# The recurrent stage of a GRU plus attention kernel is rebuilt: input part accumulated in PSUM, rows normed in row layout, no loop

## The reference, cut to what matters

```python
# x: (16, 128, 256) = B, T, D;  cond: (16, 256)
def cell(h, x_t):                                  # GRU, 128 serial steps
    i_r, i_z, i_n = split(x_t @ W_ih + b_ih, 3)    # W_ih, W_hh: (256, 768)
    h_r, h_z, h_n = split(h @ W_hh + b_hh, 3)
    r, z = sigmoid(i_r + h_r), sigmoid(i_z + h_z)
    n = tanh(i_n + r * h_n)
    return (1 - z) * n + z * h
x = x + scan(cell, cond, x over T)                 # stage 1

ada = cond @ ada_w + ada_b                         # shift1, scale1, gate1, shift2, scale2, gate2
x1 = layernorm(x) * (1 + scale1) + shift1
q, k, v = split(x1 @ qkv_w + qkv_b)                # 16 heads of 128, softmax over T = 128
y = x + gate1 * (attention(q, k, v) @ out_w + out_b)
x2 = layernorm(y) * (1 + scale2) + shift2
y = y + gate2 * (gelu(x2 @ ffn_w1 + ffn_b1) @ ffn_w2 + ffn_b2)
return x + y
```

## Time and profile before

| what | value |
|---|---|
| runs | 914.82, 917.31, 920.45 us |
| profiled execution: its own time | 920.45 us |
| its span, first to last instruction | 920.4 us |
| PE busy | 812.1 us (88%) |
| DVE busy | 621.4 us (68%) |
| ACT busy | 509.5 us (55%) |
| POOL busy | 162.2 us (18%) |
| mean granted TensorE clock | 0.881 of 2.4 GHz |

### The profile page before, as it was taken

How to read it: one execution, slowest core, us unless ns; L and a number is a source line. 1 busy time by engine, 2 the same in 40 slices (tenths; PEclk the granted TensorE clock), 3 DMA queues, 4 the chain that set the end, 5 groups by cost and what they waited for, 6 DMA issues and landing times.

```text
span 920.4 us, 29171 instructions
## 1 busy us (share of the span) xinstructions
PE 812.1 (88%) x11135; PEld 587.1 (64%) x11135; DVE 621.4 (68%) x1550; ACT 509.5 (55%) x1625; POOL 162.2 (18%) x267
## 2 busy tenths in 40 slices
PE   4985858888588878999999999999999999989998
PEld 3974747767577755676666766667766667744443
DVE  4475757777577766767767777676776778755562
ACT  3253535454345436666666666666666676664544
POOL 0043434444345430000001000000000100010130
PEclk9576767776667659999999999999999999999999
DMA  6011111112110000000000000000000000000001
GB/s 220 8 49 41 46 42 44 41 41 77 39 48 18 0 2 2 1 1 0 0 1 0 0 0 0 0 0 0 0 0 1 1 2 1 1 1 23 23 0 46
DMA packets 13257, 18.86 MB, mean 20 GB/s; under 512 B 2724, under 2 KB 9992, under 8 KB 13192
## 3 DMA queue, kind: packets, MB, share of 16 engines
q1 hardware_dynamic: 13192, 17.90, 6.4%
HBM read 15.79 MB, written 2.10 MB: 19 GB/s over the span
## 4 chain that ended last, share of the span: by engine, by line
PE 66%; DVE 14%; issue 11%; ACT 5%; SPq 1%; DMA 1%; POOL 1%; DVEq 1%; ACTq 0%; POOLq 0%
PE bank L382 15%; PE bank L384 15%; PE bank L383 15%; PE bank L501 14%; DVE nu L1068 3%; DVE h_hi L1074 3%; PE bank L635 3%; ACT zg L808 2%; DVE hs L1076 2%; DVE h_lo L1079 1%; DMA xin<-in_x 1%; PE bank L393 1%; DVE hid_lo L1156 1%; PE bank L403 1%; PE bank L458 1%
## 5 line engine op out<-in xcount | busy, mean ns | idle before, releaser
L501 PE MATMUL bank<-h_hi,whh_hi 128*128 128x16 f16 x1536 | 114.8, 178 | 19.5 <-DVE h_hi L1074 16.2
L382 PE MATMUL bank<-y_hi,w_hi 128*128 (+3 forms) x324 | 122.6, 379 | 2.4 <-DVE y_lo L1107 1.6
L383 PE MATMUL bank<-y_hi,w_lo 128*128 (+3 forms) x324 | 122.6, 379 | 0.0
L384 PE MATMUL bank<-y_lo,w_hi 128*128 (+3 forms) x324 | 122.4, 379 | 0.0
L501 PEld LDWEIGHTS bank<-h_hi,whh_hi 128*128 128x128 f16 x1536 | 93.7, 101 | 30.4 <-DVE h_hi L1074 29.6
L501 PE MATMUL bank<-h_hi,whh_lo 128*128 128x16 f16 x1536 | 112.3, 176 | 0.0
L806 ACT ACTIVATE zr<-bank 128x32 f32<-128x32 f32 x128 | 25.7, 201 | 138.7 <-PE bank L501 137.8
L884 ACT ACTIVATE prob<-bank,nmx 128x128 f32<-128x128 f32 x256 | 90.2, 364 | 10.8 <-DVE nmx L1166 10.8
L501 PEld LDWEIGHTS bank<-h_hi,whh_lo 128*128 128x128 f16 x1536 | 94.2, 102 | 0.0
L501 PE MATMUL bank<-h_lo,whh_hi 128*128 128x16 f16 x1536 | 79.7, 177 | 12.8 <-DVE h_lo L1079 12.0
L1183 DVE SCALAR_TENSOR_TENSOR kT_lo<-bank,bT,kT_hi 128x512 f16<-128x512 f32 x64 | 48.0, 750 | 63.6 <-ACT kT_hi L894 63.5
(11 more groups left out here) (177 smaller groups left out, 2451.0 us busy)
## 6 DMA issues: line engine op xcount, KB each, us to landing
stage<-in_L_cond_qkv_w SPq DMA_DIRECT2D x16, 384.0 KB, 4.8
xin<-in_x SPq DMA_DIRECT2D x128, 16.0 KB, 1.8
adaw<-in_L_cond_ada_w SPq DMA_DIRECT2D x1, 1536.0 KB, 7.4
stage<-in_L_cond_out_w SPq DMA_DIRECT2D x4, 384.0 KB, 3.5
out<-ynat SPq DMA_DIRECT2D x3, 512.0 KB, 3.0
wg<-in_L_cond_W_ih SPq DMA_DIRECT2D x1, 768.0 KB, 4.2
wg<-in_L_cond_W_hh SPq DMA_DIRECT2D x1, 768.0 KB, 5.8
stage<-in_L_cond_ffn_w SPq DMA_DIRECT2D x2, 384.0 KB, 3.6
```

What stands on the lines that cost most here:

```text
L382: mm(ps, w[0], a[0], start=start, stop=False, skip_group_check=True)
L383: mm(ps, w[1], a[0], start=False, stop=False, skip_group_check=True)
L384: return mm(ps, w[0], a[1], start=False, stop=stop, skip_group_check=True)
L501: mm = nc.tensor.matmul(out(m), half[:, k, w], a, start=False, stop=not high, skip_group_check=True)
```

## The change

The recurrent stage, its prologue and the layout of `xr` are rewritten; attention and feed-forward keep their order.

- **Gates.** Each gate has two PSUM banks that alternate by block. Bias products (with a broadcast operand) and the x_tile products of block r + 1 go straight into them, the recurrent products of the step add to them. `grz`, `gnb` and the products and evictions that moved them are gone. In a step, two z products stand ahead of the wait for `h_lo`. The n bank interleaves the hidden and the input part (every second column).
- **One place per step.** After a step's own work each engine has at most one or two pieces of other work, listed by s. x tiles come at steps 5, 6 and 7, the bias products at 1 and 2, the x transposes at 3.
- **Rows.** x is loaded with one transfer a block, partition = batch * 8 + time. The sum goes straight into `xr`, whose last axes are now (block, batch, time in the block). Mean and variance by bn_stats and bn_aggr on DVE, pow on GpSimd, two operations on DVE for scale and shift in row layout with rows of modulation, transposes back, y high and low out of PSUM in runs of eight times.
- **GpSimd** keeps the weight pieces (256 columns, five a block, each behind the step's `h_lo`) and the pow. x_low and y_low are on DVE.
- **No loop.** All 16 blocks are written out on all engines.
- **Prologue.** The small transfers are issued by ACT; the gate matrices come in halves by k and are split in quarters; the modulation is computed as rows in block 0 (shift1, scale1) and as columns in block 15 (the other eight tiles).

```diff
-        grz = [sb(f"grz{i}", [P, 2, BS, 2 * GB], f16, gru) for i in (0, 1)]
-        gnb = [sb(f"gnb{i}", [P, 2, BS, GB, 2], f16, gru) for i in (0, 1)]
...
+        r_bank, z_bank, n_bank = (bank[0], bank[3]), (bank[1], bank[6]), (bank[2], bank[7])
+        n_cols = [ps[:, :].rearrange("p (t j s) -> p t j s", t=BS, s=2) for ps in n_bank]
+        x_ps = bank[4][:, 0:D].rearrange("p (k c) -> p k c", k=KD)
+        row_ps, back_ps = bank[5][:, 0:D], bank[5][:, D:2 * D].rearrange("p (k c) -> p k c", k=KD)
...  # SP
+                sp.dma_start(xin[:, n % 2, :], x[:, n * BS:(n + 1) * BS, :]).then_inc(x_in[n % 2], 16)
+            def load_pieces(r):
+                for i in range(PB):
+                    sp.dma_start(stage[:, r % 2, i, :], pieces[r * PB + i]).then_inc(stage_in[r % 2], 16)
+            sp.dma_start(wih32[:, 0, :], wih_v[:, 0, :]).then_inc(wih_in[0], 16)
+            load_x(0)
+            sp.dma_start(wih32[:, 1, :], wih_v[:, 1, :]).then_inc(wih_in[1], 16)
...
+            for r in range(NBL - 1):
+                if r > 0:
+                    sp.wait_ge(piece_lo, r * PB)
+                load_pieces(r + 1)
+                if r + 2 < NBL:
+                    sp.wait_ge(xt_T, r + 1)
+                    load_x(r + 2)
...  # GpSimd
+            def piece_low(j, t1):
+                pool.wait_ge(piece_hi, j + 1)
+                pool.wait_ge(hlo_ok, t1 + 1)
+                r, i = j // PB, j % PB
+                gtt(w_lo[:, j * PC:(j + 1) * PC], stage[:, r % 2, i, :], w_hi[:, j * PC:(j + 1) * PC], sub
+                    ).then_inc(piece_lo, 1)
-            with pool.Fori(1, NBL - 2, 2) as r:
-                gru_block(r, 1)
-                gru_block(r + 1, 0)
+            for r in range(NBL):
+                for i, s in enumerate((1, 2, 5, 6, 7)):
+                    piece_low(r * PB + i, r * BS + (s + 1))
+                    if r > 0 and s == 2:
+                        pool.wait_ge(hlo_ok, r * BS + 5)
+                        rows_rstd(r - 1)
...  # TensorE
+            def x_bias(ps, at, width):
+                for half, first in ((bb_hi, True), (bb_lo, False)):
+                    nc.tensor.matmul(ps[:, 0:BS * width], ident16[:, :],
+                                     half[:, at:at + width].unsqueeze(1).broadcast_to([P, BS, width]), start=first,
                                      stop=False, skip_group_check=True)
...  # a step
-                pe.wait_ge(oz_ok, t1)
-                for ps, c in ((rb, 0), (zb, GB)):
...
+                pe.wait_ge(hhi_ok, t1)
+                high(0)
+                high(4)
+                high(2, slice(0, 2))
                 pe.wait_ge(hlo_ok, t1)
+                low(0).then_inc(r_mm, 1)
+                low(4).then_inc(hn_mm, 1)
+                high(2, slice(2, 8))
+                low(2).then_inc(z_mm, 1)
+            for r in range(NBL):
+                for s in range(BS):
+                    gru_step(r, s)
+                    if r > 0 and s == 0:
+                        rows_T(r - 1)
+                    if r > 0 and s == 4:
+                        rows_back(r - 1)
+                    if r < NBL - 1:
+                        if s == 1:   bias_rz(r + 1)
+                        elif s == 2: bias_n(r + 1)
+                        elif s == 3: x_block_T(r + 1)
+                        elif s == 5: (wait xt_lo) x_tile(r + 1, 0), x_tile(r + 1, 1)
+                        elif s == 6: x_tile(r + 1, 2), x_tile(r + 1, 3)
+                        elif s == 7: x_tile(r + 1, 4), x_tile(r + 1, 5)
+                    if r == 0 and s == 3:          row_modulation(0)
+                    elif r == 0 and s == 4:        row_modulation(1)
+                    elif r == NBL - 1 and s in (1, 2, 3, 4):
+                        modulation(range(2 * s + 2, 2 * s + 4))
...  # ACT, after a step's tanh
+                    if s in (0, 1, 2, 4, 6):
+                        piece_high(r * PB + (0, 1, 2, 4, 6).index(s))
+                    elif s == 3 and r < NBL - 1:
+                        x_full(r + 1)
+                        x_high(r + 1)
+                    elif s == 5 and r > 0:
                         y_high(r - 1)
...  # DVE
+            def x_low(n):
+                dve.wait_ge(xt_hi, n + 1)
+                tt(xb_lo[:, :, :].rearrange("p k (t b) -> p k t b", b=B), x_ps.rearrange("p k (b t) -> p k t b", b=B),
+                   xb_hi[:, :, :].rearrange("p k (t b) -> p k t b", b=B), ALU.subtract).then_inc(xt_lo, 1)
+            def rows_sum(n):
+                tt(xr[:, :, n, :].rearrange("p k (b t) -> p k b t", b=B),
+                   x32[:, n % 2, :, :].rearrange("p k (b t) -> p k b t", b=B),
+                   hs[:, n % 2, :, :, 1].rearrange("p t (k b) -> p k b t", b=B), ALU.add).then_inc(xr_ok, 1)
+            def rows_scale(n):
+                stt(ra[:, :], row_ps, mvb[:, 0:1], scale_rows[:, :], ALU.subtract, ALU.mult).then_inc(lb_a, 1)
+            def rows_shift(n):
+                stt(rb[:, :], ra[:, :], rsb[:, :], shift_rows[:, :], ALU.mult, ALU.add).then_inc(lb_b, 1)
+            row_work = {0: rows_sum, 1: rows_stats, 2: rows_var, 3: rows_scale, 4: rows_shift, 6: y_low}
+                    if r > 0 and s in row_work:
+                        row_work[s](r - 1)
+                    if r < NBL - 1 and s == 5:
+                        x_low(r + 1)
...  # residual (L1206); L361, L364 and L1232 in the same way
-                    op = tt(xr2[:, k, quad, :], gated[:, k, :, :], xr[:, k, quad, :], ALU.add)
+                    op = tt(by_block(xr2[:, k, quad, :]), by_block(gated[:, k, :, :]), xr_v[:, k, quad, :, :], ALU.add)
```

More of the change, by code:

```diff
@@ new lines, in _, with gru_step, high, low @@
+            bias_rz(0)
+            bias_n(0)
+            pe.wait_ge(xt_lo, 1)
+            for k in range(KD):
+                pe.wait_ge(wih_l, 2 * k + 2)
+                for m in range(GM):
+                    x_tile(0, m, (k,))
+            pe.wait_ge(whh_l, 2 * KD)
+            def gru_step(r, s):
+                t1 = r * BS + (s + 1)
+                rows = [(m, k, half) for m in range(2) for k in range(KD) for half in (whh_hi, whh_lo)]
+                def high(m0, part=slice(None)):
+                    for m, k, half in rows[part]:
+                        w = slice((m0 + m) * P, (m0 + m + 1) * P)
+                        nc.tensor.matmul(out(m0 + m), half[:, k, w], h_hi[:, k * B:(k + 1) * B, 1], start=False,
+                                         stop=False, skip_group_check=True)
+                def low(m0):
@@ L496, in gate @@
                     for m in range(2):
                         for k in range(KD):
-                            w = slice((m0 + m) * P, (m0 + m + 1) * P)
-                            a = h_hi[:, k * B:(k + 1) * B, 1] if high else h_lo[:, k * B:(k + 1) * B]
-                            for half in (whh_hi, whh_lo) if high else (whh_hi,):
-                                mm = nc.tensor.matmul(out(m), half[:, k, w], a, start=False, stop=not high,
-                                                      skip_group_check=True)
@@ L803, in gru_block @@
+            for k in range(KD):
+                gate_high(whh_hi, whh32, whh_in, whh_h, k)
+            for r in range(NBL):
                 for s in range(BS):
@@ L1048, in rows_shift @@
-            def rows_shift(n):
-                dve.wait_ge(lb_m, n + 1)
-                dve.wait_ge(lb_lo, n + 1)
-                modulate(yb, ym[:, :, :].rearrange("p k c -> p (k c)"), SH1, ALU.add, lb_y, n)
-            for half in (0, 1):
-                rz_low(0, 0, half)
-            nb_low(0, 0)
-            def gru_block(r, par, rows, ahead):
+                    tt(dst[:, :, :], ada[:, gate_tile:gate_tile + KD, :], spread(bT[:, bias:bias + KD], KD), ALU.mult
+                       ).then_inc(ada_ok, 1)
@@ L1080, in gru_block @@
-                    if s == 0 and not (isinstance(r, int) and r == 0):
-                        rz_low(r, par, 1)
-                    if rows:
-                        if s == 0:
-                            for k in range(KD):
-                                rows_sum(r - 1, 1 - par, k)
-                        elif s in rows_stage:
-                            rows_stage[s](r - 1)
-                    elif s == BS - 1:
-                        modulation()
-                    if ahead and s == 4:
-                        nb_low(r + 1, 1 - par)
@@ L1110, in rows @@
+            for work in row_work.values():
+                work(NBL - 1)
             def rows(g, j):
```

615 lines of the change are left out of this document (242 added, 373 removed).

## The result

The changed kernel took 933.91 us (median; its runs 933.09 to 934.83) beside 916.07 us for the kernel before on the same chip: a ratio of 1.021, 95% interval 1.014 to 1.028. (The ratios here leave out runs that lie more than 1.5% above the fastest of their kernel, so they can differ by up to 1% from the quotient of the medians.) The forecast was 856 us. The change made the kernel slower by about 2%, and the prediction missed by 78 us.

The account below looks back on a forecast made before the run. Bound: latency of the 128 serial steps, plus 63.0 us of excess from block 0, loop stops and GpSimd contention. The terms sum to -63.9 from the profiled 920.4, giving 856.5 us, stated as 856; range 845 to 887.

Parts of the forecast that it names:

- Part 4: Gates: removed per-step products worth 0; x tiles in steps 5 to 7 cost 0 to +9 us, taken +4.5.
- Part 6: VectorE's one work per step between h_lo and npre, window about 0.67 us: 0 to +31 us, taken +1.
- rival A: Strided reads are slow: steps 0 and 5 of each block grow by 0.75 and 1.35 us; +31, 887 us; chance 0.12.
- Part 1: Recurrent loop written out as 16 blocks, so no stops at the jump: -22.5 us.
- Part 2: Work leaves GpSimd and its weight pieces are released by h_lo, so nu is clear of contention: -32.7 us.
- Part 3: Block 0: 18 modulation products leave, -7.8 us; two row-shaped ones come in, 0 to +1.8, taken +1.
- Part 5: Two z products ahead of the h_lo wait in each step: 0 to +6.8 us in 128 steps, taken +1.
- Part 7: Block 15 takes eight modulation tiles, two per step: 0 to +1.8 us, taken +1.5.
- Part 8: Prologue: small transfers on ACT's queue, first h_hi at 13.8 to 14.3 us; -7 us, between -4 and -8.
- Part 9: Tail, up to the first last-block product: 10.3 us become about 7.4, so -2.9 us.
- Part 10: SP's issues per block fall from ten to six, 0; attention stage sums in runs of 8 floats, 0 to +8 us, taken 0.
- D: Written-out code can't be fetched in time, TensorE waits at block ends: +131, 987 us; chance 0.04.

Follow-up runs that it names:

- a: Changed kernel with rows_T issued after step 1's products instead of step 0's; 918.47 us, ratio 1.014.
- b: Changed kernel with rows_back issued after step 5's products, ahead of the tiles, instead of after step 4's; 917.97 us, ratio 1.014.
- c: Changed kernel with the six input tiles issued three each after steps 6 and 7 instead of two each after 5, 6, 7; 919.73 us, ratio 1.016.
- d: The rebalanced kernel: changed kernel with recurrent-stage work dealt out anew so no between-step TensorE wait is for same-step VectorE work; 861.86 us, ratio 0.952.
- e: Kernel before with rows_T moved from step 2 to step 0; 943.49 us, ratio 1.043.
- f: Kernel before with its recurrent-stage loop over pairs of blocks written out on all four engines; 914.42 us, ratio 1.011.
- g: d with GpSimd's five weight pieces a block no longer waiting for h_lo; 882.14 us, ratio 0.975.
- j: Changed kernel with input tiles 4 and 5 writing neighbouring columns instead of every second one, output wrong; 927.76 us, ratio 1.018.
- k: i with the two z products put back behind the low products of r and n; 852.95 us, ratio 0.935.
- i: d with the eight small loads issued ahead of the weights, four on SyncE's queue and four on ScalarE's; 857.20 us, ratio 0.947.
- the last version: i with TensorE's between-step work spread thinner and the two z products put back; 844.24 us, ratio 0.930.

## Why the prediction was wrong

**The step that failed** is in parts 4 and 6, the window that I gave each helper. TensorE's waits for VectorE's work were put at nothing, without a reason. Part 6 asked only whether VectorE's work fits between h_lo and npre, and it does (0.42 to 0.62 us). It did not ask who waits for that work. Part 4 took "TensorE's gap, behind zz and ahead of h_hi" as free room, which is right for work that has what it needs. But the gap behind step s's products lies before h_hi of step s, and the VectorE work of step s behind it. rows_T at 0, rows_back at 4 and the tiles at 5 wait for VectorE work of the same number, so TensorE reaches the wait 1.6 to 1.8 us early, and the next step's 36 products stand behind it. In the kernel before there was a step or more between each such pair. What is queued behind an added wait was named for x_low alone, and there as a bound of rival A, for the wrong reason.

The size: steps 0, 4 and 5 had 3.24, 3.34 and 4.05 where I had 2.02, 2.02 and about 2.2: 4.4 us in each of 14 blocks, 62 of the 72.5 us by which the stage was longer than the prediction's sum. The rest is block 15 (20.06 in seven periods against 15.6, with a step of 4.85), step 7 (2.40) and block 0. By stages, the profiled execution differs from the forecast by +4.6 (prologue), +72.5, -0.2 (tail) and -2.1 (what follows): 931.3 against 856.5. The cause is shown by a, b and c (each wait alone), by d, in which all three are gone (-72, 62 of them in these steps), and by e (the fault put into the old kernel, +35).

Point by point:
- Part 1, the loop: no stops in straight code, right for the profiled execution (22.3). But the -22.5 was set against one execution with three stops. The prediction saw that the stops may be what varies, and left the term as it was. Kernel f shows that they can be removed without a gain, and kernel e that an execution with the loop can have none.
- Part 2, contention: right; 193, 266 and 192 ns. g gives 20 us for five free pieces a block.
- Part 3, block 0: 19.13 where the forecast had 17.2; its step 5, with the wait for x_low, took 3.39.
- Part 4, tiles: plain ones as costed, the n tiles at twice that. So the twelve products of step 7 take 1.3 us at 2.4 GHz and 2.5 at 1.2, and its period was 2.21 to 2.32 in eleven of the 14 blocks and 2.97 to 3.09 in three. -6 us when removed (j). This is the half of rival A that came true.
- Part 5, z order: +1 was too little; putting it back gave 4.3 (k).
- Part 6, strided operands: x_low 417 ns, rows_sum 617, within the window. Rival A's other half fell. Steps 0 and 5, which A named, did grow (by 1.2 and 2.0 us), but not because these operations are slow: in d rows_sum and x_low take as long (605 and 418 ns), and the two steps have means of 2.10 and 2.02.
- Part 7, block 15: in kernel b, where no wait is mixed in, its four steps with modulation took 2.67 each, so 2.6 us against the 1.5 taken.
- Part 8, prologue: the first h_hi came at 18.71 in place of 14. "DVE: some 2.5 us of set-up" began at 10.6 us and not at about 5, for the small transfers landed at 9.90 (5.02 before) once large ones ran beside them. With them first it came at 14.59 (kernel i).
- Part 9, tail: 7.4 forecast; from 356.71 to the first last-block product 7.2.

```profile
363.92 0.18 PE L349 MATMUL bank<-y_hi,w_hi 128*128 128x32 f16 x1
```

- Part 10, the attention stage: 567.4 us from there to the end, 569.5 before. Right.

Rivals B to D did not come. D was the only one on the slower side, and its chance was 0.04; that the kernel did become slower is no point for it, for nowhere in this stage does TensorE stand over 0.5 us on "issue". None of my rivals had the mechanism that decided, though the diff shows it: to see it one has to draw one column per engine, with step numbers, and an arrow from each wait to its producer.

## What to carry to other kernels

Where one engine is in order and its work alternates between a serial chain and helpers, "in step s" means another time on each engine: write down for every wait the time at which the waiting engine reaches it and the time at which the producer ends. A helper that waits costs the chain the time from the state's arrival to the end of the wait, plus everything else queued in its gap. If it is moved one step later, the same work is free, until the gap is full (here an estimated 1.0 us: a step of 2.0 less 36 products 0.0265 apart).

And two engines that exclude each other make a schedule brittle: a shift of 0.11 us between their starts, once a block, was worth 12 us in kernel f. Release the one off the chain by an event of the chain, as the changed kernel does.

## What was not expected of the hardware

- The granted clock differs much between kernels with the same work: 0.65 of 2.4 GHz in blocks 1 to 14 of the changed kernel, 0.80 rebalanced, 0.88 in the last version. It does not simply follow the waits: kernel b, with one wait less than the changed kernel, had 0.60, and kernel k, in which only two products of each step moved, had 0.87 where its base i had 0.77. No run here isolates the cause.
- Small transfers on a queue of their own are not early if large ones are issued beside them: TensorE had them at 9.90 us, against 3.67 when half of them were issued ahead of the large ones and 5.02 when all were.
- Writing every second PSUM column doubled the spacing of 128-column products (0.11 for 0.055 at 2.4 GHz, 0.21 for 0.107 at 1.2), and left that of 16-column ones alone.
- rows_sum, with hs read at 256 bytes a step and batch and time exchanged, took 605 to 617 ns; a sum of the same size with packed output and one packed, one broadcast input (`yb`, L1039 of the kernel before) took 419. Which of its three patterns costs the time was not tried. x_low, which reads PSUM at 32 bytes a step, took 417.
